# Splitting a softmax's normalising multiplies between GpSimd and VectorE in four cross-attention layers

## The reference

```python
attn = jnp.einsum('bkhd,bnhd->bhkn', q, kmat) / DH
attn = jnp.where(full_mask[:, None, None, :], attn, -jnp.inf)
attn = jax.nn.softmax(attn.astype(jnp.float32), axis=-1).astype(q.dtype)
attn_out = jnp.einsum('bhkn,bnhd->bkhd', attn, v).reshape(b, k_len, H)
```

## Time and profile before

| | |
|---|---|
| median of 3 runs | 2568.37 us (2567.52 to 2568.99) |
| profiled execution | 2565.4 us, of it span of the trace 2563.5 us |
| TensorE busy | 2445.3 us, 95% |
| VectorE busy | 1230.3 us, 48% |
| ScalarE busy | 1083.9 us, 42% |
| GpSimd busy | 1119.2 us, 44% |
| normalising multiplies on GpSimd (L1303) | 1280 instructions |
| mean granted TensorE clock | 0.986 of full speed |

### The profile page before, as it was taken

One profiled execution on the slowest core, in us unless ns is written; L12 is line 12 of the kernel. 1 busy time (PEld: TensorE's weight loads), 2 busy tenths in 40 slices (PEclk: granted clock), 3 DMA queues, 4 the chain that ended last, 5 costly groups with the idle time before them and its releaser, 6 DMA issues.

```text
span 2563.5 us, 48757 instructions
## 1 busy us (share of the span) xinstructions
PE 2445.3 (95%) x18464; PEld 2047.5 (80%) x18464; DVE 1230.3 (48%) x3295; ACT 1083.9 (42%) x3705; POOL 1119.2 (44%) x1972
## 2 busy tenths in 40 slices
PE   6999998999999999998888999999999999899999
PEld 5888787888888878886776788888888888688887
DVE  4555655323133676766666442233455555432322
ACT  4555555111113877787677211111555555311111
POOL 2444435600044787878876640023344443730000
PEclk9999999999999999998999999999999999999999
DMA  4111222311033233223443330122021111320110
GB/s 162 59 59 59 85 74 65 96 50 50 1 96 125 87 106 120 91 102 122 139 162 127 112 99 1 50 83 78 26 87 64 51 43 59 115 87 1 50 33 17
DMA packets 106614, 198.07 MB, mean 77 GB/s; under 512 B 8272, under 2 KB 35600, under 8 KB 103312
## 3 DMA queue, kind: packets, MB, share of 16 engines
q1 hardware_dynamic: 106384, 194.97, 22.8%
HBM read 136.22 MB, written 58.72 MB: 76 GB/s over the span
## 4 chain that ended last, share of the span: by engine, by line
PE 79%; ACT 11%; DVE 5%; POOL 3%; issue 1%; DMA 0%; SPq 0%; DVEq 0%; POOLq 0%; ACTq 0%
PE banks L324 70%; ACT plain_high L714 5%; PE banks L465 5%; PE banks L495 3%; ACT plain_low L714 2%; POOL plain_high L1303 2%; DVE stats L1102 1%; ACT plain_work L779 1%; PE banks L519 1%; DVE rounded_work L1076 1%; ACT plain_work L698 1%; DVE plain_high L971 1%; DVE plain_work L1117 0%; ACT plain_low L698 0%; PE banks L454 0%
## 5 line engine op out<-in xcount | busy, mean ns | idle before, releaser
L324 PE MATMUL banks<-rounded_work,rounded_low 128*128 128x512 f32 (+1 forms) x2688 | 530.6, 353 | 23.3 <-DVE rounded_low L1131 14.0
L324 PEld LDWEIGHTS banks<-rounded_work,rounded_low 128*128 128x128 f32 x2688 | 441.6, 196 | 88.4 <-issue 16.8
L950 ACT ACTIVATE plain_work<-banks,columns 128x512 f32<-128x512 f32 x192 | 132.5, 690 | 865.3 <-PE banks L324 865.3
L324 PE MATMUL banks<-rounded_work,rounded_high 128*128 128x512 f32 (+1 forms) x2400 | 480.2, 353 | 0.4 <-DVE rounded_work L1070 0.4
L324 PEld LDWEIGHTS banks<-rounded_work,rounded_high 128*128 128x128 f32 x2400 | 393.9, 189 | 65.9 <-issue 5.5
L1303 POOL TENSOR_SCALAR plain_high<-plain_high,inv_sum 128x128 f32<-128x128 f32 (+1 forms) x768 | 296.1, 408 | 324.8 <-DVE inv_sum L993 324.4
L1279 DVE CAST rounded_work<-plain_work 128x512 fp32r<-128x512 f32 x192 | 104.7, 546 | 687.1 <-ACT plain_work L950 675.8
L324 PE MATMUL banks<-rounded_low,rounded_work 128*128 128x512 f32 x1728 | 415.1, 392 | 0.0
L324 PE MATMUL banks<-rounded_high,rounded_work 128*128 128x512 f32 (+1 forms) x1728 | 390.2, 378 | 0.0
L324 PEld LDWEIGHTS banks<-rounded_low,rounded_work 128*128 128x128 f32 x1728 | 321.7, 188 | 68.6 <-issue 2.8
L324 PEld LDWEIGHTS banks<-rounded_high,rounded_work 128*128 128x128 f32 x1728 | 309.3, 188 | 60.4 <-issue 1.4
(11 more groups left out here) (103 smaller groups left out, 3117.1 us busy)
## 6 DMA issues: line engine op xcount, KB each, us to landing
plain_work<-x SPq DMA_DIRECT2D x96, 256.0 KB, 3.3
plain_work<-mlp_w SPq DMA_DIRECT2D x96, 256.0 KB, 2.7
rounded_work<-ctx_split SPq DMA_DIRECT2D x16, 1024.0 KB, 6.0
u<-plain_work SPq DMA_DIRECT2D x48, 256.0 KB, 2.6
plain_work<-u SPq DMA_DIRECT2D x12, 1024.0 KB, 7.3
x<-plain_work SPq DMA_DIRECT2D x48, 256.0 KB, 2.2
plain_work<-attention_w SPq DMA_DIRECT2D x44, 256.0 KB, 2.6
plain_work<-inputs_t SPq DMA_DIRECT2D x8, 1024.0 KB, 7.9
```

Source lines behind the costliest of these rows:

```text
L324: mm = pe.matmul(dst, lhs(i), rhs(j), start=first and n == 0, stop=last and n == 2, skip_group_check=True)
L950: act.activation(gelu[:, j % 2, :], bank(key), ACT.Gelu_apprx_tanh, bias=col(y, 28 + j)).then_inc(evac_of(key), 1)
```

## The change

In every round GpSimd keeps banks 0 and 2. Banks 1 and 3 go to VectorE, which multiplies them right behind each half's reciprocal, inside `dve_invert`. It first waits for its own reciprocal. Per half that is one bank: two multiplies of 128 x 256 in a latent layer, four of 128 x 128 in gqa and cross. `normed` becomes two semaphores, and TensorE waits for the one of the bank's engine. Nothing else moves.

```diff
+POOL_BANKS, VECTOR_BANKS = (0, 2), (1, 3)
...
-        maxed, exped, inverted, normed = sem("maxed"), sem("exped"), sem("inverted"), sem("normed")
+        maxed, exped, inverted, normed = sem("maxed"), sem("exped"), sem("inverted"), [sem("normed_on_pool"), sem("normed_on_vector")]
...
+        def wait_normed(pe, R, r):
+            for s, banks in zip(normed, (POOL_BANKS, VECTOR_BANKS)):
+                if r in banks:
+                    pe.wait_ge(s, len(banks) * R + banks.index(r) + 1)
...
-                pe.wait_ge(normed, 4 * R + r + 1)
+                wait_normed(pe, R, r)
...
                 dve.reciprocal(inv_sum[:, R % 2, 2 * half:2 * half + 2, 0:y.segs],
                                row_sum[:, R % 2, 2 * half:2 * half + 2, 0:y.segs]).then_inc(inverted, 1)
+                for r in VECTOR_BANKS:
+                    if r // 2 == half:
+                        dve.wait_ge(inverted, 2 * R + half + 1)
+                        for g in range(y.segs):
+                            part = prob(y)[R % 2][:, r, g * y.seg:(g + 1) * y.seg]
+                            last = dve.tensor_scalar(part, part, inv_sum[:, R % 2, r, g:g + 1], None, ALU.mult)
+                        last.then_inc(normed[1], 1)
...
-            for r in range(4):
-                if r % 2 == 0:
-                    pool.wait_ge(inverted, 2 * R + r // 2 + 1)
+            for r in POOL_BANKS:
+                pool.wait_ge(inverted, 2 * R + r // 2 + 1)
                 for g in range(y.segs):
                     part = pr[:, r, g * y.seg:(g + 1) * y.seg]
                     last = pool.tensor_scalar(part, part, inv_sum[:, R % 2, r, g:g + 1], 1.0, ALU.mult, ALU.mult)
-                last.then_inc(normed, 1)
+                last.then_inc(normed[0], 1)
```

## The result

| | before | after |
|---|---|---|
| median | 2568.0 us (2567.46 to 2568.99, 5 runs) | 2600.97 us (2597.09 to 2605.54, 5 runs) |
| ratio to before, 95% interval | | 1.013 (1.0118 to 1.0141) |
| profiled execution | 2565.4 us | 2600.37 us |
| mean granted clock | 0.986 | 0.975 |

The account below looks back on a forecast made before the run. Latent layers were taken to hang on TensorE alone, gqa on four engines passing work with little room. Gqa +8.0, cross +1.3 and latent layers -4.7 gave +4.6 us: 2573.0 us, range 2566 to 2582.

Parts of the forecast that it names:

- the path and its form: In gqa, two second halves per pair lie on the chain, costing 2 x 0.73 us, less 0.3 for GpSimd's relief.
- The first half: VectorE's multiplies behind a round's first reciprocal cost nothing, covered by its wait for ScalarE's exponentials of banks 2 and 3.
- Layer 0's -2.4: Last pair of layer 0's attention: GpSimd's shorter queue ends the transposes 2.4 us earlier; layer 3 likewise, 2.3 us.
- The waits for GpSimd in the two layers: In layers 0 and 3, TensorE's waits for GpSimd's multiplies would be gone but for 2 or 3 us each.
- the step of a multiply: VectorE's price per multiply: 0.15 us for 128 x 128, bounds 0.10 and 0.25; 0.22 us for 128 x 256.
- rival C: TensorE's longer idle in gqa lowers its clock: 0 to 0.5 us a pair, a surcharge without its own chance.
- cross's steady part: In cross, a copy's 1.12 us wait for ScalarE behind the second reciprocal hides the 0.73 us shift.
- GpSimd's relief: In gqa, GpSimd loses 1.40 us of multiplies a bank; 0.2 to 0.8 us won, 0.3 taken.
- The open half: In cross's last pair the residual add follows the reciprocal at once, so the 0.73 us shift lies open.
- B: GpSimd gets between VectorE's multiplies in gqa's second halves, 0.37 us a slot: 2579 or 2585 us; chance 0.22.
- D: VectorE's bursts are hidden and GpSimd's relief is worth more: -7.7 us, 2560.7 us; chance 0.12.
- E: Cost and gain cancel within 1 us: 0.1 us a step and 0.8 gain for 0.3; 2568.4 us; chance 0.16.

Follow-up runs that it names:

- one multiply: Against the kernel before, split in gqa alone, VectorE normalising each of its banks with one multiply of 128 x 512 in place of four: 2581.58 us, ratio 1.0048.
- the run that takes the idle time away: The changed kernel, with TensorE repeating twelve transposes of bank 0 ahead of the wait in the third round of each gqa pair: 2588.79 us, ratio 1.0085.
- the run without a meeting: The changed kernel, but GpSimd starts on a half's bank only when VectorE has finished its own: 2591.0 us, ratio 1.0089.
- gqa alone: Against the kernel before, banks 1 and 3 go to VectorE only in layer 1 (gqa): 2596.35 us, ratio 1.0101.

## Why the forecast failed, point by point

**Right: the path and its form.** The forecast said that of the four halves behind a reciprocal in a pair of gqa two lie on the chain, and that a pair pays twice the shift less 0.3 us. Runs at two sizes fit it: a shift of 0.84 - 0.11 = 0.73 us (one multiply) gives 2 x 0.73 - 0.3 = 1.16, measured 48.35 - 47.3 = 1.05; the change's own shift, 1.18 - 0.11 = 1.07 us, gives 1.84, measured 49.33 - 47.3 = 2.0 where the clock stays up. The first half was free in gqa, as said, but not in cross (2 us). Layer 0's -2.4 came out as -3.3, layer 3's -2.3 as -1.1; together -4.4 for -4.7, a nearness that is partly luck. Over all traces layer 0's MLP starts at 442.5 us in the mean of the five with this split and at 444.6 in the eight without any, single ones up to 1.4 us off. The waits for GpSimd in the two layers went as said. In layer 0, where the earlier trace rows have 5.4 us, and in gqa, where they have 15.3:

```profile
PE banks L471 <- POOL plain_high L1315: 3.6, 2, 2.1
```
```profile
PE banks L471 <- DVE rounded_work L1060: 12.0, 7, 1.9
PE banks L471 <- POOL plain_high L1315: 4.9, 5, 2.3
```

In gqa the wait for GpSimd did shrink by 10 us, and the first row of the second fence took its place.

**Mis-sized: the step of a multiply.** I drew a line from an instruction of 128 x 4 at 167 ns to what I called a copy of 427 ns and took 0.15 us a step. Measured were 0.20 alone and 0.24 beside GpSimd, near the upper bound of 0.25; and the shift 1.07, where the bounds were 0.53 and 1.13. The forecast had named a step that isn't near 0.15 as a sign that it is wrong. The row at the other end was a cast, another kind of instruction, and I took its 0.51 ns an element for that of a multiply; the multiplies of 282 ns at best and 605 in the median mix two input types. For multiplies of 128 x 128 and 128 x 256 measured alone (288 and 382 ns) it is 94 ns for 128 elements, 0.73 ns an element. A pair costs 2.0 in place of 1.16, or 1.6 in place of 0.76. With the last pair that is 14.3 us (six periods of 49.33 for three of 47.7 and three of 47.3, and three halves of 1.07); what gqa's 27.5 leave beside the clock's 12.2 is 15.3, in place of 8.0.

**Dismissed: rival C.** The forecast named the wait of TensorE that would grow, and the row of the last pair where a wait of 2.2 us stands before a window at 0.66. It then counted 0 to 0.5 us a pair, since "VectorE and not TensorE ends the pair". That is the step of the prediction that failed. The stretch at the lower clock is not the transposes alone but the 36 products behind them, and these lie on the chain: 9.76 us for 5.62. The chain of before has that row in each pair too, behind the transposes. The sign that the forecast named for C, a granted clock below 1.00 in gqa's steady part, is there. Measured: 3.7 us in every second pair, and 10 to 12 us in all by the run that takes the idle time away, the largest of what the forecast had at nothing.

**Failed: cross's steady part.** The step was that a wait of 1.12 us for ScalarE hides the burst. The shift of 1.07 us nearly fills that wait, and in the run without a meeting the cast still waits 0.2 us for ScalarE behind the burst, so in those rounds it was hidden. Yet about half of the 10.2 us comes without any disturbed cast, and no run shows through which wait. The other half is lost at a place that the forecast did not look at. It treated GpSimd's relief as a gain only. The relief moves what stands behind the multiplies in GpSimd's queue, a bias add and the splitting of a tile, to earlier times, and there they meet VectorE's cast. The forecast used just this pattern for the multiplies in gqa, where it turned out small, and not for the bias add in cross, where it is large. At the end of cross it is worst; two casts of the last pair are on the chain at four times their length:

```profile
1442.33 1.03 DVE plain_low L1006 x4
1443.36 0.36 DVE rounded_work L1097
...
1445.50 1.43 DVE rounded_work L1097
...
1446.95 0.98 DVE rounded_work L1099
1447.93 1.44 DVE rounded_work L1097
```

From the end of the last exponentials to the MLP it is now 16.9 us (1442.00 to 1458.91) in place of 15.6 (1408.88 to 1424.46). The open half that the forecast placed at this end is there: the residual add starts 1.27 us behind its reciprocal (1432.36, 1431.09) in place of 0.12, so 1.15 for the 0.73 of the sum. What it lacked was the half behind it.

**The other rivals.** B blamed the excess on GpSimd between VectorE's multiplies, 0.37 us a slot: the run without a meeting moved the burst by 0.15 us and the time by 10 us, part of it where the casts of cross are undisturbed; it left 23 us to explain. D is out by the sign. E is out too, and its sum was wrong: with a shift of 0.53 and a gain of 0.8 a pair the forecast's own terms give 2 for gqa and 0.9 for cross, so -1.9 and 2566.5, not 2568.4.

**The sum again,** with the measured terms in place of the forecast's: 4.6 + 7.3 (step and shift in gqa, 15.3 for 8.0) + 12.2 (clock) + 8.9 (cross, 10.2 for 1.3) + 0.3 (latent layers) = 33.3 us; measured 33.0. That it closes is no proof, since 15.3 is itself what was left over. Built up from the parts, gqa has 14.3 for the delay and 3 x 3.7 for its three slow rows, 25.4 of the 27.5; the other 2 us, at the ends of the stage, are not accounted for. With the right price of the step, near its upper bound, and nothing else changed the forecast would have been some 2580, still 21 us short. The terms that were missing are larger than the one that was wrong.

## What to carry to other kernels

Before a delay on one engine is priced at its size, look at what TensorE does behind the wait that it lengthens: if products on the chain follow there, the lower clock is a price of its own, here 10 to 12 us beside 15 for the delay. Work taken off an engine moves up everything that is queued behind it; go through that queue and ask what each step will now run beside. And what costs here is the place and not the amount: the first half's bank moved for nothing in gqa and for 2 us in cross, while four idle instructions behind the second half cost as much as moving its work.

## What the runs showed of the hardware

The granted clock after an idle TensorE in gqa. With waits of 1.90 us (the change) it fell in every second pair, with 1.76 and 1.84 us in every second or third, with 1.57 us (the one multiply) in two pairs of eight, with 1.45 us in one, and with 0.61 us, or the 0.85 of before, in none. From 1.57 us on, a full fall stretched 36 products on the chain from 5.62 us to between 9.3 and 10.1; the one at 1.45 us made its pair only 0.4 longer. What decides that one pair is hit and the next, with the same wait, is not, these runs don't tell. It differs between executions too: of gqa alone, the one at a mean granted clock of 0.980 took 2587.8 us, the three at 0.974 to 0.976 took 2594.4 to 2599.0.

How GpSimd and VectorE disturb each other depends on the pair of instructions. VectorE's cast of 128 x 512 (0.43 us alone) beside GpSimd's add of two tensors took 1.27 to 1.46 us and ended 0.29 us after the add. Beside GpSimd's idle multiplies of 128 x 384 it took 0.51, beside its multiplies of 128 x 128 in the run without a meeting 0.43, while these took 0.71 us each (2.83 for four) and not 0.35. A burst of four of VectorE's multiplies beside GpSimd's took 1.03 for 0.88; one of 128 x 256 on VectorE took 479 ns for 382, on GpSimd some 560 for 486. The Trainium skill (SBUF — State Buffer, "Who interferes with whom") says that who issues second "fully blocks": with that the trace of the add agrees. The multiplies differ, and here the measurement decides: the rule would make VectorE wait out one of GpSimd's, of 0.41 us in this trace, and the runs show 0.15 on a burst of four, with both engines slowed.
